# Two weight folds as three fp32r products, the first weights in four pieces, and a new order of the opening

## The reference

```python
x = x + cross_attention(layernorm(x), ctx, ctx, mask, gamma, beta)   # ctx: 16 x 1601 x 512
x = x + self_attention(layernorm(x), W_qkv, W_out)
x = x + experts(layernorm(x), router_w, expert_w1, expert_w2)        # 8 experts, 2 per row, 2048 wide
```

```python
y = einsum('bsh,oh->bso', x, W_qkv).reshape(*x.shape, 3)
q, k, v = y[..., 0], y[..., 1], y[..., 2]
attn = softmax(einsum('bqh,bkh->bqk', q, k) * scale)
out = einsum('bsh,oh->bso', einsum('bqk,bkh->bqh', attn, v), W_out)
```

## Time and profile before

| | |
|---|---|
| median of three executions | 802.03 us |
| the profiled execution's own time | 801.91 us |
| its span | 800.3 us |
| TensorE products busy | 740.5 us, 93% |
| VectorE busy | 447.5 us, 56% |
| ScalarE busy | 304.8 us, 38% |
| GpSimd busy | 148.5 us, 19% |
| read from memory | 188.16 MB |

### The profile page before, as it was taken

One profiled execution on the slowest core, in us unless ns is written; L12 is line 12 of the kernel. 1 busy time (PEld: TensorE's weight loads), 2 busy tenths in 40 slices (PEclk: granted clock), 3 DMA queues, 4 the chain that ended last, 5 costly groups with the idle time before them and its releaser, 6 DMA issues.

```text
span 800.3 us, 12058 instructions
## 1 busy us (share of the span) xinstructions
PE 740.5 (93%) x4626; PEld 552.3 (69%) x4626; DVE 447.5 (56%) x1052; ACT 304.8 (38%) x508; POOL 148.5 (19%) x160
## 2 busy tenths in 40 slices
PE   5999899999999999862999899999999999999992
PEld 3453345364545453442999899999999998888882
DVE  4153467676868646755456544555556655566520
ACT  2031112122221211221555354556565565656620
POOL 2133030412213010104201021111210212120201
PEclk9999999999999999985899999999999999999997
DMA  9999999999999999211254455564755757674402
GB/s 340 401 421 383 421 384 384 418 379 423 381 421 367 421 412 400 120 52 35 88 163 183 119 176 186 141 208 161 209 189 170 208 205 205 215 235 167 122 1 27
DMA packets 35133, 198.85 MB, mean 248 GB/s; under 512 B 4540, under 2 KB 4924, under 8 KB 14080
## 3 DMA queue, kind: packets, MB, share of 16 engines
q1 hardware_dynamic: 29680, 187.81, 61.8%
q0 software_dynamic: 4672, 9.11, 6.1%
q10 hardware_dynamic: 720, 1.10, 0.4%
HBM read 188.16 MB, written 9.85 MB: 247 GB/s over the span
## 4 chain that ended last, share of the span: by engine, by line
PE 77%; DVE 8%; DMA 7%; issue 3%; SPq 2%; ACT 1%; POOL 1%; POOLq 0%; DVEq 0%; ACTq 0%
PE ps L756 8%; PE ps L985 8%; PE ps L797 8%; PE ps L987 8%; PE ps L986 8%; PE ps L1007 4%; PE ps L1008 4%; PE ps L1009 4%; PE ps L1014 4%; PE ps L1015 4%; PE ps L1016 4%; DMA arena<-in_w_out 3%; DMA arena<-in_ctx_turned 3%; PE ps L812 3%; PE ps L827 3%
## 5 line engine op out<-in xcount | busy, mean ns | idle before, releaser
L459 POOL TENSOR_TENSOR small<-small 128x1 f32<-128x1 f32 x64 | 20.9, 327 | 618.3 <-DVE yb_space L1510 198.0
L987 PE MATMUL ps<-xT,low_a 128*128 128x288 f32 (+5 forms) x384 | 111.1, 289 | 0.0
L1482 DVE TENSOR_TENSOR h_ring<-hid,h_ring 128x288 fp32r<-128x288 f32 (+5 forms) x128 | 55.6, 435 | 96.4 <-ACT h_ring L1173 93.4
L1168 ACT ACTIVATE hid<-ps 128x288 f32<-128x288 f32 (+5 forms) x128 | 50.6, 395 | 151.2 <-PE ps L987 148.7
L797 PE MATMUL ps<-arena 128*64 128x512 f32 (+1 forms) x416 | 94.5, 598 | 3.0 <-DMA arena<-in_ctx 1.8
L1371 DVE TENSOR_TENSOR low_a<-w_raw_a,high_b 128x2048 fp32r<-128x2048 f32 x32 | 73.2, 2291 | 37.7 <-ACT high_b L1108 36.4
L1061 ACT COPY arena<-ps 128x512 f32<-128x512 f32 (+2 forms) x93 | 43.8, 528 | 122.9 <-PE ps L731 66.7
L756 PE MATMUL ps<-arena 128*64 128x512 f32 x384 | 85.5, 596 | 0.9 <-DMA arena<-in_ctx_turned 0.7
L985 PE MATMUL ps<-xT,high_b 128*128 128x288 f32 (+5 forms) x256 | 74.9, 292 | 0.0
L987 PEld LDWEIGHTS ps<-xT,low_a 128*128 128x128 f32 x384 | 73.5, 191 | 0.0
L986 PE MATMUL ps<-xT,high_b 128*128 128x288 f32 (+5 forms) x256 | 73.4, 287 | 0.0
(11 more groups left out here) (192 smaller groups left out, 1615.7 us busy)
## 6 DMA issues: line engine op xcount, KB each, us to landing
arena<-in_ctx_turned SPq DMA_DIRECT2D x48, 1024.0 KB, 23.3
arena<-in_ctx SPq DMA_DIRECT2D x48, 1024.0 KB, 22.7
w_raw_a<-in_w SPq DMA_DIRECT2D x48, 1024.0 KB, 5.0
w_raw_b<-in_w SPq DMA_DIRECT2D x16, 1024.0 KB, 4.9
arena<-in_mask SPq DMA_DIRECT2D x8, 800.5 KB, 26.8
arena<-in_w_qkv SPq DMA_DIRECT2D x3, 1024.0 KB, 9.4
arena<-in_ctx SPq DMA_DIRECT2D x16, 130.0 KB
out<-res SPq DMA_DIRECT2D x8, 256.0 KB, 22.1
```

Of the source, the lines that this page charges most:

```text
L987: mm = pe.matmul(o, w_low[2 * f][:, cols], high[:, k, 0:w.width], start=False, stop=(k == KC - 1))
L1168: nc.scalar.activation(hid[:, c % 2, 0:w.width], bank(c % UP_BANKS)[:, 0:w.width], ACT.Gelu).then_inc(gelu_done, 1)
L1482: dve.tensor_tensor(h_ring[:, c % RING, 1, 0:w.width], hid[:, c % 2, 0:w.width], h_ring[:, c % RING, 0, 0:w.width].bitcast(F32), ALU.subtr ...
```

## The change

- `fold` takes a high and a low part of each side, in fp32r, and makes three products per piece (high by high, high by low, low by high) in place of one in fp32. The four parts have new tiles, `fold_high` and `fold_low`.
- For wq, wk and wv ScalarE copies all four fills to the high part, and VectorE then subtracts this from the bank to give the low part; only the second frees the bank. The output weights are split in the same way, without turning.
- The query weights come in four pieces with a semaphore each. TensorE turns piece by piece into all four banks. x of tile 0 is issued behind the key weights.
- The value and output weights are issued after the first fold has ended, not after the key weights are turned.
- The value weights are turned between tile 0's second and third block of scores. The second fold comes after tile 1's query and rest.
- VectorE does `queries(1)` before `softmax(0)`, whose two maskings are taken apart; ScalarE's copies for tile 1 come before the exponentials of tile 0.

```diff
-    for kind in ("xq", "rest0", "rest1", "qr"):
+    for kind in ("xq", "rest0", "rest1"):
         yield kind, 0, 0
-    for which in ("wv", "vo"):
-        for n in range(KC):
-            yield which, 0, n
+    for n in range(KC):
+        yield "wv", 0, n
+    yield "qr", 0, 0
     for kind in ("xq", "rest0", "rest1"):
         yield kind, 1, 0
+    for n in range(KC):
+        yield "vo", 0, n
...
-    return n % 2 == 0 if kind in ("wq", "wk", "m") else kind not in ("out", "qr", "logit", "rank", "pt")
+    return n % 2 == 0 if kind == "m" else kind not in ("wq", "wk", "wv", "out", "qr", "logit", "rank", "pt")
...
+            for k in range(KC):
+                sp.dma_start(raw_q[:, k, :], w_qkv[:, k * D:(k + 1) * D]).then_inc(wq_in[k], 16)
+            sp.dma_start(raw_k, w_qkv[:, WBLK:2 * WBLK].rearrange("p (k h) -> p k h", k=KC)).then_inc(wk_in, 16)
             sp.dma_start(res[:, 0:D], x[0:P, :]).then_inc(x_in, 16)
-            sp.dma_start(raw_q, w_qkv[:, 0:WBLK].rearrange("p (k h) -> p k h", k=KC)).then_inc(wq_in, 16)
-            sp.dma_start(raw_k, w_qkv[:, WBLK:2 * WBLK].rearrange("p (k h) -> p k h", k=KC)).then_inc(wk_in, 16)
...
-            sp.wait_ge(filled, filled_at("wk", 0, KC - 1))
+            sp.wait_ge(filled, filled_at("m", 0, KC - 1))
...
-            def fold(kind, left, right):
+            def fold(kind, high_left, low_left, high_right, low_right):
...
-                        mm = pe.matmul(o, left[:, hc, m * P:(m + 1) * P], right[:, hc, :],
-                                       start=(hc == 0), stop=(hc == KC - 1))
+                        pe.matmul(o, high_left[:, hc, cols], high_right[:, hc, :], start=(hc == 0), stop=False)
+                        pe.matmul(o, high_left[:, hc, cols], low_right[:, hc, :], start=False, stop=False)
+                        mm = pe.matmul(o, low_left[:, hc, cols], high_right[:, hc, :], start=False, stop=(hc == KC - 1))
...
-            pe.wait_ge(wq_in, 16)
-            for hc in range(KC):
-                turn_weights("wq", raw_q, hc)
+            for k in range(KC):
+                pe.wait_ge(wq_in[k], 16)
+                for hc in range(KC):
+                    o = open_fill("wq", 0, hc)
+                    mm = pe.transpose(o[:, k * P:(k + 1) * P], raw_q[:, k, hc * P:(hc + 1) * P], ident)
+                    if k == KC - 1:
+                        mm.then_inc(filled, 1)
...
-            for blk in range(NBLK - 1):
-                scores(0, blk)
-            rest_scores(0)
+            scores(0, 0)
+            scores(0, 1)
             pe.wait_ge(wv_in, 16)
             for hc in range(KC):
                 turn_weights("wv", raw_v, hc)
-            pe.wait_ge(wo_in, 16)
-            wait_copied(pe, "wv", 0, KC - 1)
-            fold("vo", turned_v, raw_out)
+            scores(0, 2)
+            rest_scores(0)
             turn_query(1)
             turn_rest(1)
+            wait_copied(pe, "wv", 0, KC - 1)
+            pe.wait_ge(out_split, 1)
+            fold("vo", high_v, low_v, high_out, low_out)
...
+            def high_fill(kind, dst):
+
+                for n in range(KC):
+                    act.wait_ge(filled, filled_at(kind, 0, n))
+                    act.copy(dst[:, n, :], bank(bank_at(kind, 0, n))).then_inc(turned_high, 1)
...
+            act.wait_ge(wo_in, 16)
+            act.copy(high_out, raw_out).then_inc(out_high, 1)
+            high_fill("wv", high_v)
+            copy_query(1)
+            copy_rest(1)
             exps(0)
             for n in range(KC):
                 copy_fill("vo", 0, values_w[:, n, :], n)
-            copy_query(1)
-            copy_rest(1)
...
+            def low_fill(kind, count, low, high):
+
+                dve.wait_ge(filled, filled_at(kind, 0, KC - 1))
+                for n in range(KC):
+                    dve.wait_ge(turned_high, count + n + 1)
+                    dve.tensor_tensor(low[:, n, :], bank(bank_at(kind, 0, n)), high[:, n, :].bitcast(F32), ALU.subtract
+                                      ).then_inc(copied[False], 1)
...
-            for kind, dst in (("wq", turned_q), ("wk", turned_k), ("m", scores_w)):
-                for n in range(1, KC, 2):
-                    copy_fill(kind, n, dst[:, n, :])
+            low_fill("wq", 0, low_q, high_q)
+            low_fill("wk", KC, low_k, high_k)
+            for n in range(1, KC, 2):
+                copy_fill("m", n, scores_w[:, n, :])
+            queries(1)
+            dve.wait_ge(out_high, 1)
+            dve.tensor_tensor(low_out, raw_out, high_out.bitcast(F32), ALU.subtract).then_inc(out_split, 1)
+            masked_scores(0, 0)
+            low_fill("wv", 2 * KC, low_v, high_v)
+            masked_scores(0, 1)
             softmax(0)
-            queries(1)
```

More of the change, by code:

```diff
@@ L255, in build @@
             pass
+        with (nc.sbuf_tensor("before_folds", [P, 17408], F32), nc.sbuf_tensor("fold_low", [P, 2, KC, D], F32R) as fold_low,
+              nc.sbuf_tensor("fold_high", [P, 2, KC, D], F32R) as fold_high):
+            pass
         high_c = sb("high_c", [P, 2, WBLK], F32R)
@@ L313, in build @@
         raw_q, raw_k = [view(17408 + i * WBLK, KC, D) for i in range(2)]
-        turned_q, turned_k = [view(21504 + i * WBLK, KC, D) for i in range(2)]
-        raw_v, raw_out, turned_v = raw_q, raw_k, turned_q
+        raw_v, raw_out = raw_q, raw_k
+        low_q, low_k = [fold_low[:, i, :, :] for i in range(2)]
+        high_q, high_k = [fold_high[:, i, :, :] for i in range(2)]
+        low_v, low_out, high_v, high_out = low_q, low_k, high_q, high_k
         probT = view(37888, CHUNKS, P)
@@ L382, in build @@
         x_in, x1_in, x_rest_in, cst_in, gb_in = sem("x_in"), sem("x1_in"), sem("x_rest_in"), sem("cst_in"), sem("gb_in")
-        wq_in, wk_in, wv_in, wo_in, rw_in = sem("wq_in"), sem("wk_in"), sem("wv_in"), sem("wo_in"), sem("rw_in")
+        wq_in = [sem(f"wq_in{k}") for k in range(KC)]
+        turned_high, out_high, out_split = sem("turned_high"), sem("out_high"), sem("out_split")
+        wk_in, wv_in, wo_in, rw_in = sem("wk_in"), sem("wv_in"), sem("wo_in"), sem("rw_in")
         ctx_here = [sem(f"ctx_here{b}") for b in range(NBLK - 1)]
@@ L717, in turn_weights @@
                 mm.then_inc(filled, 1)
-            def fold(kind, left, right):
+            def fold(kind, high_left, low_left, high_right, low_right):
                 for m in range(KC):
                     o = open_fill(kind, 0, m)
+                    cols = slice(m * P, (m + 1) * P)
                     for hc in range(KC):
-                        mm = pe.matmul(o, left[:, hc, m * P:(m + 1) * P], right[:, hc, :],
-                                       start=(hc == 0), stop=(hc == KC - 1))
+                        pe.matmul(o, high_left[:, hc, cols], high_right[:, hc, :], start=(hc == 0), stop=False)
+                        pe.matmul(o, high_left[:, hc, cols], low_right[:, hc, :], start=False, stop=False)
+                        mm = pe.matmul(o, low_left[:, hc, cols], high_right[:, hc, :], start=False, stop=(hc == KC - 1))
                     mm.then_inc(filled, 1)
@@ L869, in _ @@
                 wait_copied(pe, "wk", 0, n)
-            fold("m", turned_q, turned_k)
+            fold("m", high_q, low_q, high_k, low_k)
             turn_query(0)
             turn_rest(0)
-            for blk in range(NBLK - 1):
-                scores(0, blk)
-            rest_scores(0)
+            scores(0, 0)
+            scores(0, 1)
             pe.wait_ge(wv_in, 16)
@@ L1115, in _ @@
             act.wait_ge(cst_in, 16)
-            for kind, dst in (("wq", turned_q), ("wk", turned_k), ("m", scores_w)):
-                for n in range(0, KC, 2):
-                    copy_fill(kind, 0, dst[:, n, :], n)
+            def high_fill(kind, dst):
+                for n in range(KC):
+                    act.wait_ge(filled, filled_at(kind, 0, n))
+                    act.copy(dst[:, n, :], bank(bank_at(kind, 0, n))).then_inc(turned_high, 1)
+            high_fill("wq", high_q)
+            high_fill("wk", high_k)
+            for n in range(0, KC, 2):
+                copy_fill("m", 0, scores_w[:, n, :], n)
             copy_query(0)
             copy_rest(0)
-            for n in range(KC):
-                copy_fill("wv", 0, turned_v[:, n, :], n)
+            act.wait_ge(wo_in, 16)
[3 more added lines that the diff above has]
+            copy_rest(1)
             exps(0)
@@ L1259, in queries, with masked_scores @@
                 normalize(xq, tile_of(p)).then_inc(xq_ready, 1)
-            def softmax(j):
+            def masked_scores(j, part):
                 dve.wait_ge(bound_ready, j + 1)
@@ L1264, in softmax @@
                     dve.wait_ge(filled, filled_at("p", j - 1, NBLK - 1))
[L1265 to L1268, removed]
+                a, b, blk = ((0, 2 * BLK, 1), (2 * BLK, 3 * BLK, 2))[part]
+                dve.wait_ge(scored, scored_at(j, blk))
```

(6 more changed lines are left out.)

## The result

The kernel after took 815.66 us (815.10 to 816.55, four executions) against 801.98 of the kernel before (801.83 to 803.76): the ratio is 1.0168, 95% interval 1.0153 to 1.0183. That is 13.7 us slower; the forecast was 9.5 slower, 811.4, and its range ended at 814.5. The profiled execution has a span of 814.5 us (800.3 before).

A forecast was written before the change was run, and what follows sets the result against it. Transfers bound the kernel up to 96 us, TensorE afterwards. Tile 0's probabilities come 12.0 us later, less 2.5 forgiven, so 9.5 on 801.9 gives 811.4 us; stated range 804.5 to 814.5.

The forecast's parts named there:

- dry queue: Value weights wait for the first fold, so DMA engines run dry for about 7 us; both weights landed at about 50.6.
- Order on the SP queue: Tile 0's x, behind 2 MB of weights, lands at about 11.3 us in place of 4.5, 6.8 later; pieces worth nothing.
- VectorE's opening: VectorE's work before the low parts, held by GpSimd's mask operation until 21.9 us; first low part 23.8, bounds 18.6 and 25.1.
- Splitting: ScalarE's high parts, then VectorE's low parts, of query and key weights: from 23.8 us to the first fold at 30.0.
- Products and clock: Both folds: 48 products at 0.232 us, 11.1 each, 2.6 less per fold; low clock adds 2.0 to the first.
- Between the folds: Tile 0 scores, value and output weights: first fold ends at 43.1 us, weights land at 50.6, second fold starts at 59.5.
- What is forgiven: TensorE's three waits for transfers after the second fold, 2.48 us together, vanish and give back that much of the lateness.
- Rival C: More is lost: line 606 adds 1.3 us, or waits for context blocks return; 11 to 13 slower, 814; chance 0.15.

The follow-up runs named there:

- late-x run: Kernel before, with x rows of tiles 3 to 7 (1.3 MB) issued behind tile 2's turned context: 800.2 us, ratio 0.9978 to the kernel before.

## Why the prediction was right in kind and too small

The forecast's chain held link by link: x late, VectorE's opening late, held by GpSimd, low parts, fold, a dry queue, later weights, some 2.5 us forgiven. The sizes did not: 13.7 us slower in place of 9.5. Two terms at the head of the chain made most of the difference.

- *Order on the SP queue: the step that failed.* "The sum of bytes up to there is the same, so x lands at about 11.3 us." It landed at 15.2. The bytes were the same, the rate was not: the pieces slowed the queue. With one transfer it landed at 11.6, in the kernel before with x behind at 11.4: the step was right without the pieces. I had priced the pieces as an early start that is worth nothing and costs nothing. The same slower queue broke a second sentence, that the mask's landing "is not moved": its operation started at 18.64, not 16.24. It is by the mask's delay that the pieces reached the first low part: 27.3, and 25.2 with one transfer.
- *VectorE's opening.* Holding by the mask operation was right. The addition of line 606 holds as well; I had kept it out of the forecast as a bound, and it was the true case in every kernel in which x was behind the weights and the mask operation was not moved: 1.39 us on line 1418 or its like in three, 1.07 in the kernel before with x behind. The first low part started at 27.3, forecast 23.8: of these 3.5 us, 2.1 are the pieces, 1.2 are line 606.
- *Splitting.* Forecast 6.2 us from the first low part to the fold, measured 6.9. The sum was inconsistent with its own pace: four groups of four transposes at 0.205 us take 3.3 us, so that the last cannot be done 2.8 us after the end of the first low part, as the forecast had it. They took 3.42.
- *Products and clock.* The first fold took 12.6 us (13.1 forecast), the third to the tenth product 0.43 apart, the later ones 0.227; the window below has the clock at 0.56. The second took 11.0. The figure of the Trainium skill, "TensorE: Matmul & The Clock Gate", section "Wait — 56ns, not 53.3ns?", 215.7 ns, was too low by 11 ns here; the row of 0.232 was too high by 5. The first transposes of the kernel before, which I had read as a row of the low level, have a granted clock of 1.00 from 7.8 to 11.0 us: that they are slow is measured, that the clock makes them slow is not shown.
- *Between the folds.* The second fold started 17.1 us after the end of the first, forecast 16.4: the output weights landed 8.5 us after that end, forecast 7.5.
- *What is forgiven.* Forecast 2.48; 3.0 up to tile 2's last block. No wait but 0.30 was left, as forecast. The late-x run in the kernel before confirms that transfers bound that part: moving 1.3 MB out of their way gave 0.22%.

ScalarE's row for the output weights, and then two windows of the first fold:

```profile
55.31 1.90 ACT L1146 CAST fold_high<-arena 128x2048 fp32r<-128x2048 f32 x1 [6.73 <-DMA arena<-in_w_out]
```

```profile
34.20:38.00 3.80, 3.78 (x10) 2.98 (x11) 0.00 (x0) 0.00 (x0) 0.00 (x0) 0.56 0.79 265
38.10:46.80 8.70, 8.70 (x39) 7.12 (x39) 0.69 (x1) 1.18 (x2) 0.00 (x0) 1.00 0.03 10
```

These windows show the hole in the transfers as well: 10 GB/s from 38 to 47 us.

The probabilities are turned at 74.9, forecast 70.6. These 4.3 us are 3.5 up to the first low part, 0.7 of splitting, 0.7 between the folds, less 0.6 of the folds. The forecast of the time is short by 4.3 as well, and that the two agree so closely is partly luck: 0.5 more was forgiven than I had counted, the profiled execution lost 0.9 again later, and it is itself 0.5 above the median. Rival C had the sign and the term (line 606) but also leaned on waits for context blocks, which did not come.

## What to carry to other kernels

Before a small transfer is moved behind large ones, ask which engine's whole program begins with it; here 256 KB of x gated everything that VectorE did, and moving them cost 8 us (kernel after), 10 (with whole weights) or 12 (kernel before). Price a cut of a transfer by its rate, and for all that stands behind it, not only by when its first piece is there. And when a stretch of one engine shifts in time, look what it now runs into: here GpSimd's mask operation of tile 0 and the addition behind it, which met nothing of VectorE's before, cost 4 us.

## What the runs showed of the hardware that was not expected

- Four transfers of 256 KB in place of one of 1 MB lowered the rate from 4 to 6 and 6 to 8 us from 409 and 429 GB/s to 354 and 304 (cut by columns) and 242 and 260 (cut by 32 partitions), at a DMA share of 1.03 to 1.11 (0.99 and 1.03 with one transfer).
- A VectorE operation in SBUF of 72 elements a partition, 0.16 or 0.23 us otherwise, took 3.87 to 5.58 us beside GpSimd's mask operation and 1.39 beside its addition; a subtraction of SBUF from PSUM was not held (2.48 us for four, with and without). One with two SBUF inputs was let go before the mask operation ended: in the kernel before it took 3.97 us from 45.84, up to 49.81, and the mask operation ran from 45.65 to 51.29.
- In the kernel after, the third to the tenth product of the first fold ran at the low level (0.43 us apart, granted clock 0.56 from 34.2 to 38.0 us), after 3.42 us of turning and a wait of 2.62. In the kernel before, whose fold followed its turning after 0.83 us, the granted clock from 14.8 to 18.0 us is 1.00 and no record is slow.
